# AdaLN block with memory attention: norms on column tiles, the fourth combination in the query phase, and the first query product directly behind the last bank products

## What is computed

```python
h = layernorm(x) * (1 + ca) + sa
q = (h @ Wq.T) in 16 heads of 32;  sigma_q = elu(q) + 1
a_unnorm = einsum('bhsd,nhde->nbhse', sigma_q, memories)       # 4 memory banks n
norm     = einsum('bhsd,nhd->nbhs',  sigma_q, memory_norms)
a        = a_unnorm / clip(norm, 1e-6)[..., None] * active
combined = einsum('nbhse,hn->bhse', a, softmax(bank_weights))
x = x + ga * (combined @ Wo.T)
h = layernorm(x) * (1 + cb) + sb
g = silu(h @ w_gate) * (h @ w_up)            # 2048 hidden, of each 4 the 2 largest by size are kept
x = x + gb * (sparsified(g) @ w_down)
```

## Time and profile before

| what | us |
|---|---|
| median of 3 runs | 1416.51 |
| lowest, highest | 1416.03, 1418.0 |
| the profiled execution's own time | 1417.38 |
| its span, first to last instruction | 1415.6 |
| PE busy in it | 1381.5 (98%) |
| DVE busy | 877.4 (62%) |
| ACT busy | 507.5 (36%) |
| POOL busy | 560.7 (40%) |

### The profile page before, as it was taken

How to read it: one execution, slowest core, us unless ns; L and a number is a source line. 1 busy time by engine, 2 the same in 40 slices (tenths; PEclk the granted TensorE clock), 3 DMA queues, 4 the chain that set the end, 5 groups by cost and what they waited for, 6 DMA issues and landing times.

```text
span 1415.6 us, 18994 instructions
## 1 busy us (share of the span) xinstructions
PE 1381.5 (98%) x6998; PEld 1147.0 (81%) x6998; DVE 877.4 (62%) x1275; ACT 507.5 (36%) x797; POOL 560.7 (40%) x395
## 2 busy tenths in 40 slices
PE   7999999998999999999999999999999999999998
PEld 5788888887788888888888888788888888888887
DVE  6787777778594645455555656574545555564637
ACT  5466676665633222222122234342222212222211
POOL 1755665666073313132331346471313133132312
PEclk9799999999999999999999999999999999999999
DMA  6303112213420202011010302230201101020102
GB/s 247 121 30 119 72 77 89 89 59 120 178 97 1 97 0 96 30 67 63 33 67 30 126 30 97 90 126 1 97 29 67 64 33 67 30 96 0 67 0 97
DMA packets 24127, 102.44 MB, mean 72 GB/s; under 512 B 2688, under 2 KB 3232, under 8 KB 14496
## 3 DMA queue, kind: packets, MB, share of 16 engines
q1 hardware_dynamic: 24096, 102.05, 19.4%
HBM read 68.47 MB, written 33.57 MB: 72 GB/s over the span
## 4 chain that ended last, share of the span: by engine, by line
PE 83%; DVE 10%; ACT 3%; issue 2%; DMA 1%; POOL 0%; SPq 0%; ACTq 0%; DVEq 0%
PE bank L1150 26%; PE bank L1152 25%; PE bank L1151 25%; PE bank L1224 2%; PE bank L1174 2%; DVE banks_r L968 1%; PE bank L1205 1%; DVE h_abs L1095 1%; DVE ln_raw L798 1%; PE bank L1234 1%; DVE pair_lo L1077 1%; ACT h_full L528 1%; DMA x_ring<-in_x_dram 1%; DVE both_of L1080 1%; DVE x_ring L931 0%
## 5 line engine op out<-in xcount | busy, mean ns | idle before, releaser
L1054 DVE TENSOR_TENSOR h_act<-bank,silu_g 128x512 f32<-128x512 f32 x128 | 88.0, 690 | 403.4 <-PE bank L1152 382.2
L462 POOL TENSOR_TENSOR hs_lo<-h_abs,hs_hi 128x512 fp32r<-128x512 f32 x124 | 170.0, 1400 | 378.6 <-ACT hs_hi L691 378.6
L412 POOL TENSOR_TENSOR h_lo<-h_raw,h_hi 128x512 fp32r<-128x512 f32 x64 | 124.7, 1976 | 233.7 <-ACT h_hi L674 233.7
L1150 PE MATMUL bank<-h_hi,up_w_hi 128*128 128x512 f32 x512 | 199.7, 390 | 3.6 <-POOL up_w_lo L456 2.0
L1150 PE MATMUL bank<-h_hi,gate_w_hi 128*128 128x512 f32 x512 | 199.7, 390 | 0.6 <-ACT silu_g L706 0.5
L1152 PE MATMUL bank<-h_hi,gate_w_lo 128*128 128x512 f32 x512 | 199.2, 389 | 0.0
L1152 PE MATMUL bank<-h_hi,up_w_lo 128*128 128x512 f32 x512 | 199.2, 389 | 0.0
L1151 PE MATMUL bank<-h_lo,up_w_hi 128*128 128x512 f32 x512 | 199.2, 389 | 0.0
L1151 PE MATMUL bank<-h_lo,gate_w_hi 128*128 128x512 f32 x512 | 199.2, 389 | 0.0
L706 ACT ACTIVATE silu_g<-bank 128x512 f32<-128x512 f32 x128 | 76.0, 596 | 329.3 <-PE bank L1152 329.3
L1150 PE MATMUL bank<-down_w_hi,hs_hi 128*128 128x512 f32 x496 | 192.9, 389 | 0.0
(11 more groups left out here) (142 smaller groups left out, 2442.7 us busy)
## 6 DMA issues: line engine op xcount, KB each, us to landing
h_raw<-h2T_scratch SPq DMA_DIRECT2D x16, 1024.0 KB, 4.8
x_ring<-in_x_dram SPq DMA_DIRECT2D x8, 1024.0 KB, 5.5
x_scratch<-x_ring SPq DMA_DIRECT2D x8, 1024.0 KB, 3.9
h2T_scratch<-h_full SPq DMA_DIRECT2D x8, 1024.0 KB, 3.9
over_x<-x_scratch SPq DMA_DIRECT2D x8, 1024.0 KB, 4.8
acc_scratch<-over_x SPq DMA_DIRECT2D x8, 1024.0 KB, 3.9
over_x<-acc_scratch SPq DMA_DIRECT2D x8, 1024.0 KB, 4.9
out_dram<-over_x SPq DMA_DIRECT2D x7, 1024.0 KB, 3.9
```

The lines of the kernel that those rows point to most:

```text
L412: nc.gpsimd.tensor_tensor(h2_lo[:, k], h2_raw[:, k], h2_hi[:, k].bitcast(F32), ALU.subtract).then_inc(h2_lo_done, 1)
L462: nc.gpsimd.tensor_tensor(hs_lo[:, j], h_abs[:, j], hs_hi[:, j].bitcast(F32), ALU.subtract).then_inc(hs_lo_done, 1)
L1054: nc.vector.tensor_tensor(h_act[:, cc, j], bank[2 * (j % 2) + 1][:], silu_g[:, j % 2], ALU.mult).then_inc(h_done, 1)
L1150: nc.tensor.matmul(out_, stat[0], mov[0], start=start, stop=False)
```

## The change

1. **Norms.** `norms(u, s)` is gone from all four subtiles. `norm_products(t)` makes the norms of all 512 tokens at once: for each g, the norm table (128 x 32, padded with zeros) is the stationary operand, on the column tile that writes partitions 32g to 32g + 31, and sigma (128 x 512, fp32) is the moving one. The result is in bank 7. ACT copies it to `norm_rows` (`norm_copy`). PE transposes it back, four transposes into bank 6 (`norm_transposes`), which stand between the two halves of `banks_of(t, 0)`. DVE inverts in two parts: subtile 0, then subtiles 1 to 3 at once (`invert_norms(t, 0)`, `(t, 1)`), both ahead of the scaling of subtile 1.
2. **Fourth combination.** `comb_transpose(u+3)` moves from the next tile's start to between `q_block` 2 and 3, with ACT's `combT_high` and DVE's `combT_low` for it.
3. **First query product.** `q_block(t+1, 0)` stands directly behind `banks_of(t, 3)`, ahead of `wo_product(u+1)`. So `t2` 0 and 1, the combination and `t2` 2 and 3 now follow one another.
4. `t1(t+1, 0)` and 1 stand ahead of `comb_transpose(u)` and banks 2. ACT's `h1_split` is cut in two, the first part at s = 1. The statistics of `attn_rest(t, 0)` come after the scaling of subtile 3 (`late_stats`).

Tile 0 keeps the old place of `t1` and `q_block` 0, tile 7 has neither. The diff, cut to its core:

```diff
-            norm_bd = sba("norm_bd", [P, K, NB, HG])
+            norm_bd = sba("norm_bd", [P, K, DH])
+            norm_rows = sba("norm_rows", [P, T])
-            inv_norm = sba("inv_norm", [P, 2, K * NB * HG])
+            inv_norm = sba("inv_norm", [P, S, K, NB * HG])
...
+            def norm_copy(t):
+                act.wait_ge(norm_done, 4 * t + 4)
+                nc.scalar.activation(norm_rows[:], bank[7][:], ACT.Copy).then_inc(norm_rows_done, 1)
...
                     if s == 0:
-                        transposed()
+                        norm_copy(t)
...
                     if s == 1:
-                        transposed()
+                        if first or last:
+                            transposed()
+                        else:
+                            h1_split(t + 1, before_last=transposed, part=0)
...
-                            h1_split(t + 1, before_last=transposed)
+                            h1_split(t + 1, before_last=transposed, part=None if first else 1)
...
-                    sigma_all(t + 1, between=h2_rest)
+                    sigma_all(t + 1, between=h2_rest, before_high=lambda: combT_high(4 * t + 3, 1))
...
+            def invert_norms(t, part):
+                subs = (slice(0, 1), slice(1, S))[part]
+                inv = inv_norm[:, subs]
+                dve.wait_ge(normT_done, 4 * t + 4)
+                if t > 0:
+                    dve.wait_ge(banks_r_done, 4 * (4 * (t - 1) + subs.stop))
+                found = bank[6][:].rearrange("p (s g c) -> p s g c", s=S, g=K)[:, subs, :, 0:NB * HG]
+                nc.vector.tensor_scalar(inv, found, NORM_EPS, None, ALU.max).then_inc(clip_done, 1)
+                dve.wait_ge(clip_done, 2 * t + part + 1)
+                nc.vector.reciprocal(inv, inv).then_inc(recip_done, 1)
...
                     sigma_of(t, 2)
+                    combT_low(u - 1, 1)
...
-                    attn_rest(t - 1, 2, u - 2, between=lambda: combT_low(u - 1, 1))
-                    invert_norms(u, 0)
+                    attn_rest(t - 1, 2, u - 2)
+                    invert_norms(t, 0)
                     next_scalars()
                     scale_banks(u, 0)
 
-                invert_norms(u + 1, 1, first)
+                invert_norms(t, 1)
                 if first:
                     next_scalars()
                 scale_banks(u + 1, 1, first)
-                invert_norms(u + 2, 0, first)
...
-                attn_rest(t, 0, u, between=lambda: combT_low(u + 1, 1))
-
-                invert_norms(u + 3, 1, first)
+                attn_rest(t, 0, u, between=lambda: combT_low(u + 1, 1), stats=False)
+
                 scale_banks(u + 3, 1, first)
+                late_stats(t, 0, u)
...
+            def norm_products(t):
                 for g in range(K):
+                    nc.tensor.matmul(bank[7][DH * g:DH * (g + 1), :], norm_bd[:, g], sigma[:, g],
+                                     start=True, stop=True).then_inc(norm_done, 1)
+
+            def norm_transposes(t):
+                pe.wait_ge(norm_rows_done, t + 1)
+                for s in range(S):
+                    toks = slice(s * P, (s + 1) * P)
+                    nc.tensor.transpose(bank[6][:, toks], norm_rows[:, toks], ident[:]).then_inc(normT_done, 1)
...
                 if not first:
                     wo_product(u - 2, 0)
-                    comb_transpose(u - 1)
                 pe.wait_ge(sigma_done, 4 * t + 4)
                 if first:
                     pe.wait_ge(norm_bd_ready, 1)
-                norms(u, 0)
-                banks_of(t, 0)
+                norm_products(t)
+                banks_of(t, 0, between=lambda: norm_transposes(t))
...
+                def t1_first():
+                    pe.wait_ge(clip_done, 2 * t + 2)
+                    t1(t + 1, 0)
+                    if first:
+                        pe.wait_ge(rows_done, 3)
+                    t1(t + 1, 1)
+
+                if not first and not last:
+                    t1_first()
...
                 comb_transpose(u, first=first)
                 banks_of(t, 2)
...
-                norms(u + 3, 3)
                 banks_of(t, 3)
+                if not first and not last:
+                    q_block(t + 1, 0)
                 wo_product(u + 1, 1)
...
-                else:
+                elif first:
                     q_block(t + 1, 0)
...
                     for g in range(1, K):
                         q_block(t + 1, g)
+                        if g == 2:
+                            comb_transpose(u + 3)
```

More of the change, by code:

```diff
@@ L522, in ln_sqrt, with h1_split @@
                 nc.scalar.activation(ln_sd[:, which], ln_var[:, which], ACT.Sqrt).then_inc(sd_done[which], 1)
-            def h1_split(t, first=False, before_last=lambda: None):
+            def h1_split(t, first=False, before_last=lambda: None, part=None):
                 def full(k):
@@ L535, in hi @@
                     nc.scalar.activation(h1_hi[:, k], h1_full[:, k], ACT.Copy).then_inc(h1_hi_done, 1)
[L537 to L549, removed]
+                if part != 1:
+                    full(0)
+                    if first:
+                        hi(0)
+                    full(1)
+                    if part == 0:
+                        before_last()
+                    if not first:
+                        act.wait_ge(q_done, 4 * t)
+                        hi(0)
+                    hi(1)
+                if part != 0:
+                    full(2)
+                    hi(2)
+                    full(3)
+                    before_last()
+                    hi(3)
             def h2_affine(t, first=False, blocks=range(K)):
@@ L944, in split_w_low @@
                 nc.vector.tensor_tensor(lo[:], raw, hi[:].bitcast(F32), ALU.subtract).then_inc(w_lo_dve, 1)
[L946 to L954, removed]
+            def invert_norms(t, part):
[7 more added lines that the diff above has]
+                dve.wait_ge(clip_done, 2 * t + part + 1)
                 nc.vector.reciprocal(inv, inv).then_inc(recip_done, 1)
             def scale_banks(u, s, first=False):
-                inv = inv_norm[:, s % 2]
                 if not (first and s < 2):
                     dve.wait_ge(comb_done, u - 1)
-                dve.wait_ge(recip_done, u + 1)
+                dve.wait_ge(recip_done, 2 * (u // S) + min(u % S, 1) + 1)
                 scaled = banks_r[s % 2][:].rearrange("p k n c -> p (k n c)").rearrange(
                     "p (g i b a e) -> p g i b a e", g=2, i=2, b=PAIR, e=DH)
-                r = inv.rearrange("p (g i b a) -> p g i b a", g=2, i=2, b=PAIR)
+                r = inv_norm[:, u % S].rearrange("p (g i) (b a) -> p g i b a", g=2, b=PAIR)
                 for g in range(K):
@@ L1200, in q_block, with banks_of @@
                 ins.then_inc(q_done, 1)
[L1202 removed]
+            def norm_products(t):
                 for g in range(K):
[L1204 to L1209 removed]
+                    nc.tensor.matmul(bank[7][DH * g:DH * (g + 1), :], norm_bd[:, g], sigma[:, g],
[5 more added lines that the diff above has]
+                    nc.tensor.transpose(bank[6][:, toks], norm_rows[:, toks], ident[:]).then_inc(normT_done, 1)
+            def banks_of(t, s, between=lambda: None):
                 u = 4 * t + s
@@ L1227, in banks_of @@
                                     ins.then_inc(banks_done, 1)
+                    if two == 0:
+                        between()
             def comb_transpose(u, first=False):
@@ L1284, in tile @@
                     wo_product(u - 1, 1)
-                pe.wait_ge(clip_done, u + 1)
-                norms(u + 1, 1)
                 banks_of(t, 1)
-                pe.wait_ge(clip_done, u + 2)
-                norms(u + 2, 2)
+                def t1_first():
+                    pe.wait_ge(clip_done, 2 * t + 2)
+                    t1(t + 1, 0)
+                    if first:
+                        pe.wait_ge(rows_done, 3)
+                    t1(t + 1, 1)
+                if not first and not last:
+                    t1_first()
                 if first:
@@ L1294, in tile @@
                 banks_of(t, 2)
-                if not last:
-                    pe.wait_ge(clip_done, u + 3)
-                    t1(t + 1, 0)
-                    if first:
-                        pe.wait_ge(rows_done, 3)
-                    t1(t + 1, 1)
+                if first:
+                    t1_first()
                 if first:
@@ L1320, in tile @@
                 else:
-                    pe.wait_ge(clip_done, u + 4)
+                    if last:
+                        pe.wait_ge(clip_done, 2 * t + 2)
+                    else:
+                        pe.wait_ge(h1_full_done, 4 * (t + 1) + 3)
                     t2(t - 1, 0)
```

29 lines of the change are left out of this document (11 added, 18 removed).

## The result

The changed kernel takes **1422.71 us** (median of 7 runs, 1419.87 to 1425.41) against 1416.51 for the kernel before (7 runs, 1415.92 to 1418.0): ratio 1.004, 95% interval 1.0031 to 1.005. That is 6.2 us slower, more than the 2.8 us that a measurement tells from no change. The forecast was no difference, 1418.5, with a range of 1408 to 1427.

What follows compares the result with a forecast made beforehand. PE, busy 98% of the span, was taken as the bound, its savings paid back as waits on other engines. 0.4 + 6 x 0.4 - 0.75 = +2.05 us on the median 1416.51 gave 1418.5 us; range 1408 to 1427.

Steps and rivals of the forecast that it cites:

- The other two signs: Prediction wrong if the second scaling starts over 0.5 us from +10.5, or if h1_lo ends before +24.
- the lock: Rival: POOL holds up DVE's ln_shift before x1 of u; 1.15 us more a tile, 1425.5 us; chance 0.17.
- the clock: Rival: new PE waits in the loop bring another 20.5 us at half clock, up to 10 us, 1428; chance 0.03.
- the first tile: Three inversions delay the second scaling by about 1 us, and the moved combination is added: +0.4 us.
- the rivals that the range took in: DVE held up by POOL (chance 0.17, 1425.5 us) and half of the faster case (chance 0.15, 1408 for half).
- that estimate by slope: DVE's inversion of subtiles 1 to 3, from per-column and per-element costs: clip 0.34 us, reciprocal 1.35 us.
- that rival: Norm products on column tiles don't run side by side: 1.2 to 2.4 us more a tile, 1427 to 1435; chance 0.07.
- The x1 wait: PE at the output product of u waits 1.0 us for DVE's x1 of u-1, from +13.95 to +14.95.
- The second norm's wait: PE waits 0.8 us at the second norm's transposes, whose gap `q_block` 0 had covered.
- the 0.2 that I had taken: Norm transposes cut the bank products in two; moves between tiling modes cost 0 to 0.2 us a tile, 0.2 taken.
- a floor of 36.4: PE's looped tile with 2.2 us less work and its waits gone: 36.4 us, from 39.60.
- the last tile: PE waits for DVE's x1 anyway; that x1 comes 0.75 us earlier and what follows hangs on it: -0.75 us.

Runs made afterwards that it cites:

- after: The changed kernel itself, with all four parts, against the kernel before: 1422.71 us, ratio 1.004.
- q0_back: The changed kernel with `q_block` 0 of the next tile back in its old place, behind the combination of subtile 2: 1410.64 us, ratio 0.9957.
- norms_only: The changed kernel with parts 2, 3 and 4 undone, only the norms on column tiles left: 1416.82 us, ratio 1.0002.
- q0_mid: The changed kernel with `q_block` 0 one place later, behind `wo_product(u+1)` and still ahead of `t2`: 1415.6 us, ratio 0.9992.
- q0_only: The kernel before with `q_block` 0 alone put ahead, directly behind the bank products of subtile 3: 1441.73 us, ratio 1.0182.
- shift_late: The changed kernel with DVE's layer-norm scalars for the second norm behind the scaling of subtile 3, in all tiles: 1424.96 us, ratio 1.0056.
- shift_loop: The changed kernel with DVE's second-norm scalars behind the scaling of subtile 3 in the looped tiles only: 1420.85 us, ratio 1.003.
- after_novar: The changed kernel without DVE's `ln_var`, eps going in as the bias of ACT's square root: 1420.79 us, ratio 1.0027.
- norms_t1: norms_only with part 4 (`t1` ahead of banks 2, late statistics) put on it: 1413.41 us, ratio 0.9984.
- back_both: q0_back without `ln_var` and with the reciprocals of subtiles 2 and 3 moved behind x1 of u-1: 1407.41 us, ratio 0.993.
- back_split: q0_back with the reciprocals of subtiles 2 and 3 moved behind x1 of u-1 on DVE: 1414.78 us, ratio 0.9989.
- back_novar: q0_back without DVE's `ln_var`, eps going in as the bias of ACT's square root: 1409.04 us, ratio 0.9944.

## Why the prediction came out as it did

**The sign.** The range held the time; the forecast of no difference didn't hold. By one of its own signs the prediction was wrong too: it said so for a loop that changes by over 1 us a tile, and the profiled loop changed by 1.16 (6.95 over six). The other two signs kept within their bounds (second scaling +10.73, last h1_lo +24.95). In the profiled run, +8.0 is made of: six tiles at +0.6, 3.6 us (I had 2.4); the lock in three, 1.7; the clock fall, 1.6; the first tile, 1.4 (I had 0.4); the last, -0.2 (I had -0.75); 0.2 less in the rest. That the time lay within 1408 to 1427 is owed to the rivals that the range took in, not to the sum.

**Right, by rows of after.** The plain tile, one without the lock and the clock fall: 40.20 against 40.0. Its chain, as offsets from +0 = 163.38: second scaling +10.73 (said +10.54), with the clip of 192 columns 0.35 us (0.34) and the reciprocal 1.35 (1.35), so that estimate by slope held. The norm products 1.00 us (0.96): they run side by side, and that rival is out. The x1 wait 0.91 (1.0). `q_block` 0 starts at +22.38 (+22.4) and its fourth h1_lo is there at +24.95 (+24.63); PE waits 1.55 us in it (1.4). The second norm's wait showed too, 0.32 us as idle time, and 0.29 more within the second pair of transposes, which take 1.08 us (193.72 to the next start at 194.80) where q0_back's take 0.79.

**Slightly short: the plain tile, 0.2 us.** The first scaling began at +6.50 instead of +6.32, and POOL's sums at +12.09 instead of +11.91. A chain that is serial passes such a lateness on whole; POOL's own chain took 12.86 us instead of 12.72, and the fourth h1_lo was 0.32 late. The bank products of subtile 0 took 1.82 us in two halves, against 1.63, the 0.2 that I had taken. That the Trainium skill (TensorEngine Tiling (Array Packing), Key Properties) has a drain at each change of mode fits; by zero drain the sum would have been 0.4 us short of the 40.20 instead of 0.2. The norm transposes, between two such changes, took 0.59 us (168.10 to 168.69) where I had 0.44.

**Too large: what PE saves.** I had 2.2 us a tile, and a floor of 36.4. PE's busy time fell from 38.57 us to 37.4 in the plain tile, to 37.0 in norms_only and 36.65 in q0_back. The two terms above are a part of the difference; the 0.29 within the second pair of transposes is a wait that counts as busy. The rest I didn't part. The waits, in turn, were 2.8 us and not 3.5: none shows at the first combination, where I had 0.3.

**Mis-sized: the lock.** I had it as a rival (0.17) that would act in all six tiles for 1.15 us each. It acted in three, for 0.58. The mechanism was as told, at the instruction that I named. The size was off because the plain tile waits for the fourth h1_lo anyway: with the lock, `q_block` 0 starts at +23.55, runs through and ends at +26.4, where it ends at +25.8 without it. In kernels where POOL is not the next in line the same loss costs its full 1.2 us (q0_back, q0_mid). What I put as a condition, "over 0.15 us later than I have it", was met by the +0.2 above, and the gap was still won three times. What I gave as a threshold was in fact a matter of which of two starts comes first in a gap of a few hundredths of a us; that it went three and three in the profiled run is chance as far as the rows show.

**Mis-sized: the clock.** I gave it 0.03 and priced a stretch like the one of 20.5 us before the loop. The wait ahead of it is not one of those of 0.8 to 1.4 us that I listed, but the 2.4 us that the lock makes of the 1.28. The two rivals were not independent. In the loop the stretch is 3.4 us, its price 1.2 (q0_only) to 1.6 us, where I had up to 10.

**First and last tile.** Of the first's +1.4 I had 0.4; 0.35 is there before the norms of the first tile run (the modulation row starts at 36.81). In q0_back, q0_mid, shift_late and shift_loop the first tile's code is that of after, and their first stretch ends at 80.85 to 81.18, +0.4 to +0.75. So after's +1.4 is for the most part this execution's own, and the +0.4 may stand. The stretches at half clock before the loop lie elsewhere in after than in these executions. In the last tile PE runs at half clock for 10.2 us from 346.8, before for 6.8 from 341.4. In shift_loop and after_novar, without such a stretch, the same part takes 86.91 and 86.53 us. So the -0.75 may well be there under the clock's loss; as the kernel before had such a stretch too, no run parts them.

**What the sum hid.** The prediction gave one sum for four edits that pull apart: nothing for part 1, nothing for part 2 on top of it, -1.2 for part 4 on top of it, +1.85 for part 3. Its own working had the pieces: it named the gap between the second-norm transposes whose cover goes, and both waits of `q_block` 0. What it didn't ask is what the tile would be with the product left where it was: 38.35.

## What to carry to other kernels

Where several engines' chains are within a us of each other, taking work from the busiest one turns into waits (norms_only: 1.6 us of work out, nothing gained) until the order lets the next chain start earlier (part 4, with `t1` ahead of banks 2: 1.2 us). A product that needs the last results of two other engines is the filler to put behind everything that needs less; put first, it pays their lateness and leaves bare the gap it had covered. Cost each part of a change by itself, also against the version that lacks it: a sum near zero can be two effects of opposite sign, and the better kernel is one of them.

## What was new about the hardware

- A DVE instruction of 128x4 that takes 0.16 us alone took 1.32 behind a POOL instruction when it began in the gap between two of them, in 3 of 6 tiles of after (in q0_mid in 2 of 6, in q0_back, norms_t1 and back_both in 1, in back_split in none); arriving in the middle of one it took 0.94 to 0.97 in each (back_novar, after_novar).
- `ln_var`, with one input, 128x4 fp32, was held too: 1.07 to 1.09 us in every looped tile of after, 0.17 before at 215.91. The kernel before has such a case as well: its `ln_var` at the start of a tile (at 199.09) began within POOL's `sigma_lo` and took 0.80.
- The clock fell to 0.50 behind single waits of 1.9 to 2.4 us amid otherwise dense work of the loop, each time for 3.4 us: in after behind one of three such waits, in q0_mid behind one of two, in q0_only behind five of six. In q0_back, norms_t1 and back_both one wait of 1.8 to 2.0 us each brought none, and neither did a wait of 2.8 us in shift_loop's last tile.
- Four fp32 products of 32 output rows by 512 columns, each the only one on its column tile, take 1.00 us together. A reciprocal on DVE took 1.35 us for 192 elements a partition, 0.95 for 128 (back_split) and 0.55 for 64: about 6.3 ns an element.
